# Rest blocks of the experts: 64 rows standing twice in the array instead of 128 rows once

## The chip, the cores and the metric

The kernel runs on one core of one Trainium2 chip. The metric is the device time of one execution in microseconds, lower is better; the median of several runs is compared. TensorE is called PE in the profile, its weight loads PEld, VectorE DVE, ScalarE ACT, GpSimd POOL and SyncE SP.

## The reference, cut to what matters

A decoder layer: causal self-attention, a mixing step over features, and a layer of 64 experts. Only the last part is touched. Each of the 4096 tokens goes to 8 experts; an expert computes a SiLU-gated product of two projections and projects it back, and the result is added to the token with its weight.

```python
logits = x @ gate_weight.T
top_val, top_idx = lax.top_k(softmax(logits), 8)        # 64 experts, 8 for each token
...
gu = lax.ragged_dot(xs, swapaxes(gate_up_proj, 1, 2), group_sizes)   # rows x 1024 by 1024 x 768
gate, up = jnp.split(gu, 2, axis=-1)
hact = jax.nn.silu(gate) * up
y = lax.ragged_dot(hact, swapaxes(down_proj, 1, 2), group_sizes)     # rows x 384 by 384 x 1024
out = zeros_like(x).at[tok].add(y * w[:, None])
```

4096 x 8 rows over 64 experts are 512 for each on average. Worked out from the reference and its inputs: 30 of the 64 experts get more than 512 rows. Their surplus over 512 is 145 rows for expert 0; 65, 95, 109 and 84 rows for experts 11, 29, 45 and 59; and 1 to 64 rows for the other 25. No expert is remapped.

## The kernel before, in words

All products are in fp32 made of two parts: a number is split into an upper part (`_hi`) and a remainder (`_lo`), and a product is three matmuls, upper by upper, upper by remainder, remainder by upper (`split_product`, L1931 to L1934).

The expert stage is `experts`. `for_experts` (L1802 to L1812) runs on each engine: for each expert one **super block** of 512 rows (`super_block`), then as many **rest blocks** (`tail_block`) as the expert has rows beyond 512, in pieces of 128 (`route` counts them into `blocks` and `starts`). Each engine's order is written out by hand, and engines meet only through semaphores.

A rest block on PE (L2024 to L2063): `first_layer(f)` for the three thirds f of the inner dimension, each 8 x 3 matmuls of 256 columns into `ps_gu` with the 128 rows as the stationary operand; `turn_h(f)` transposes the activation; `turn_tail` transposes the rows of the next gather (`xt_rows`); `second_layer(f)` makes 2 x 3 matmuls of 512 columns into `ps_y`. ACT makes the SiLU (L2163) and the upper parts of the transposed activation (L2168) and of the gathered rows (`split_tail`, L2085), DVE the product (L2355) and the remainders (L2359, L2259).

The result of a block leaves `ps_y` only when the next block runs: ACT scales it into `y_last` (`finish_last`, L2094), and POOL adds its 128 rows to `out` with one indirect DMA (`send_last`, L1897). The fourth piece of a super block goes the same way. POOL also gathers the rows of the next block (`gather_tail`, L1878). The row numbers of the send stand in `scatter_l`. DVE writes them for the next send as the last thing that it does in a rest block (L2375 to L2377), once `yl_sent` tells that the running send has landed.

After a rest block DVE goes on with the next expert, and the first thing there is the remainder `gu_lo` of its weights (`first_weights`, L2291), after ACT's upper part `gu_hi` (L2114). The first matmul of PE's next super block waits for the first piece of it.

The rows of each expert are listed on DVE in `table` (`finish_list`, L2218 to L2231), one column for each block of 128 rows.

## Time and profile before

| | us |
|---|---|
| median of 3 runs | 7708.75 (7703.13 to 7712.73) |
| profiled execution, its own time | 7711.42 |
| span of its instructions | 7709.8 |
| expert stage, from its first matmul | 3728.4 to the end |
| super blocks | 64 |
| rest blocks | 31 (93 transposes on L2044, three for each) |

The page gives each engine's busy time and the granted clock of PE in 40 slices of the span. The timeline gives single instructions with start and duration in us from the span's start, and in square brackets how long the engine was idle before and what released it. A duration of a matmul is longer than its distance to the next one, since matmuls are pipelined; what counts is the distance of the starts.

### The profile page before, as it was taken

Reading aid. Unit: us, or ns where it says so; the run is one execution under the profiler, and the core shown is the slowest. Engines: PE = TensorE matmul, PEld = TensorE weight load, DVE = VectorE, ACT = ScalarE, POOL = GpSimd, SP = SyncE. Lnnn points to the kernel's source line nnn. Section 1 sums busy time; section 2 is a strip of 40 time slices with the busy share of each in tenths; the row PEclk is TensorE's granted clock in tenths of the full one; section 3 lists DMA queues with packets and bytes.
Section 4 is the critical chain, followed back from the end, with each engine's and each line's share of the span. In section 5 each row is a group of like instructions: output and inputs, shape, how many; then the busy total and the mean of one; then the engine's idle time right before and its main releaser. Section 6 shows DMA issues by size and latency. Waiting matters only on the chain.

```text
span 7709.8 us, 118231 instructions
## 1 busy us (share of the span) xinstructions
PE 7148.1 (93%) x37743; PEld 5881.9 (76%) x37744; DVE 3972.6 (52%) x7056; ACT 3523.7 (46%) x6510; POOL 1815.6 (24%) x1602
## 2 busy tenths in 40 slices
PE   7998888898996899995799999999999999999999
PEld 5776776776775778784688888888888888888887
DVE  5666667666665443445444444444444444444444
ACT  4666676666665222120244444444444444444443
POOL 1122113113110000000233333333333333333333
PEclk9999999999998999996899999999999999999999
DMA  2111111112111222221465555556556565556555
GB/s 66 45 55 51 44 55 51 44 45 60 45 46 58 79 69 85 76 67 36 123 176 170 161 161 161 161 161 165 161 155 165 161 181 160 159 163 162 162 161 150
DMA packets 303596, 858.60 MB, mean 111 GB/s; under 512 B 42080, under 2 KB 83552, under 8 KB 303328
## 3 DMA queue, kind: packets, MB, share of 16 engines
q0 software_dynamic: 98928, 365.58, 20.3%
q1 hardware_dynamic: 204400, 489.67, 19.5%
q8 instruction: 142, 2.33, 0.1%
q14 instruction: 126, 1.03, 0.0%
HBM read 614.84 MB, written 206.70 MB: 107 GB/s over the span
## 4 chain that ended last, share of the span: by engine, by line
PE 52%; DVE 0%; POOL 0%; issue 0%; DMA 0%; ACT 0%; DVEq 0%; POOLq 0%
PE ps_gu L1932 10%; PE ps_gu L1934 10%; PE ps_gu L1933 10%; PE ps_y L1932 5%; PE ps_y L1934 5%; PE ps_y L1933 5%; PE ps_xe L1952 3%; PE ps_xe L1961 1%; PE ps_l L1941 1%; PE ps_h L2044 0%; DVE logits L2206 0%; DMA x_rows<-rows,gather_s 0%; DVE xs_lo L2252 0%; DVE at_hi L2199 0%; POOL x_rows L1869 0%
## 5 line engine op out<-in xcount | busy, mean ns | idle before, releaser
L1932 PE MATMUL ps_gu<-xs_hi,gu_hi 128*128 128x512 f32 x3072 | 1213.5, 395 | 7.3 <-DVE gu_lo L2291 7.3
L1934 PE MATMUL ps_gu<-xs_hi,gu_lo 128*128 128x512 f32 x3072 | 1207.0, 393 | 0.0
L1933 PE MATMUL ps_gu<-xs_lo,gu_hi 128*128 128x512 f32 x3072 | 1204.4, 392 | 0.0
L1911 POOL TENSOR_TENSOR dn_lo<-raw_w,dn_hi 128x512 fp32r<-128x512 f32 x384 | 485.0, 1298 | 947.0 <-ACT dn_hi L2114 947.0
L1932 PEld LDWEIGHTS ps_gu<-xs_hi,gu_hi 128*128 128x128 f32 x3072 | 577.8, 188 | 130.4 <-DVE gu_lo L2291 7.7
L461 PE MATMUL ps_qkv<-xt_hi,w_hi 128*128 128x512 f32 x1512 | 639.8, 423 | 37.7 <-ACT proj L614 30.0
L1933 PEld LDWEIGHTS ps_gu<-xs_lo,gu_hi 128*128 128x128 f32 x3072 | 578.1, 188 | 124.8
L1934 PEld LDWEIGHTS ps_gu<-xs_hi,gu_lo 128*128 128x128 f32 x3072 | 577.6, 188 | 125.3
L1932 PE MATMUL ps_y<-dn_hi,hs_hi 128*128 128x512 f32 x1536 | 628.6, 409 | 0.0
L893 DVE TENSOR_TENSOR pt_lo<-ps_t,pt_hi 128x512 fp32r<-128x512 f32 (+3 forms) x768 | 426.6, 555 | 391.9 <-ACT pt_hi L713 376.9
L644 ACT ACTIVATE probs<-ps_s,neg_max 128x128 f32<-128x128 f32 (+7 forms) x512 | 379.5, 741 | 506.6 <-DVE neg_max L824 505.7
L461 PE MATMUL ps_qkv<-xt_lo,w_hi 128*128 128x512 f32 x1512 | 610.6, 404 | 0.0
L2126 ACT ACTIVATE hs_hi<-act_s 128x512 fp32r<-128x512 f32 x192 | 121.3, 632 | 1067.8 <-DVE act_s L2301 1067.8
L461 PE MATMUL ps_qkv<-xt_hi,w_lo 128*128 128x512 f32 x1512 | 607.1, 402 | 0.0
L1934 PE MATMUL ps_y<-dn_hi,hs_lo 128*128 128x512 f32 x1536 | 606.6, 395 | 0.0
L1933 PE MATMUL ps_y<-dn_lo,hs_hi 128*128 128x512 f32 x1536 | 606.0, 395 | 0.0
L2301 DVE TENSOR_TENSOR act_s<-ps_gu,act_s 128x512 f32<-128x512 f32 x192 | 132.8, 691 | 894.2 <-PE ps_gu L1934 894.2
L2252 DVE TENSOR_TENSOR xs_lo<-ps_xe,xs_hi 128x512 fp32r<-128x512 f32 x520 | 334.3, 684 | 478.5 <-ACT xs_hi L2077 478.5
L1889 POOL DMA_INDIRECT out<-y_sup,scatter_s x192 | 303.1, 1579 | 1012.2 <-ACT y_sup L2136 983.1
L2291 DVE TENSOR_TENSOR gu_lo<-raw_w,gu_hi 128x512 fp32r<-128x512 f32 x768 | 485.1, 686 | 102.3 <-ACT gu_hi L2114 101.9
L2114 ACT ACTIVATE gu_hi<-raw_w 128x512 fp32r<-128x512 f32 x768 | 427.2, 620 | 218.7 <-DMA raw_w<-w_gu 159.8
L544 PE MATMUL ps_t<-ident,probs 128*128 128x128 f32 x2304 | 393.3, 281 | 78.5 <-ACT probs L652 54.9
(326 smaller groups left out, 15577.1 us busy)
## 6 DMA issues: line engine op xcount, KB each, us to landing
raw_w<-w_gu SPq DMA_DIRECT2D x384, 512.0 KB, 4.2
raw_w<-w_down SPq DMA_DIRECT2D x192, 512.0 KB, 6.3
w_raw<-wqkv SPq DMA_DIRECT2D x192, 256.0 KB, 2.7
turned<-proj SPq DMA_DIRECT2D x512, 64.0 KB, 2.0
out<-residual SPq DMA_DIRECT2D x36, 512.0 KB, 2.6
attn_out<-out_t POOLq DMA_DIRECT2D x128, 128.0 KB, 2.3
residual<-x SPq DMA_DIRECT2D x32, 512.0 KB, 5.3
stage<-attn_out SPq DMA_DIRECT2D x32, 512.0 KB, 5.8
```

The costliest lines, as they stand in the source:

```text
L461: mm = pe.matmul(out[:, :], ws[:, kind, k, :], xs[:, k, a], start=(n == 0), stop=(n == 3 * HB - 1))
L544: mm = pe.transpose(ps_t[:, (1 + at) % 2, i * P:(i + 1) * P], probs[g][:, i, kb * P:(kb + 1) * P], ident[:, :])
L644: act.activation(probs[g][:, i, 0:keys], ps_s[:, n % 2, 0:keys], ACT.Exp, bias=neg_max[:, n:n + 1], accum_out=row_sum[:, n:n + 1]).then_in ...
L893: dve.tensor_tensor(pt_lo[:, s % 2, off:], ps_t[:, (1 + at) % 2, off:], raw(pt_hi[:, s % 2, off:]), ALU.subtract).then_inc(tile_lo_ok, 1)
L1889: pool.indirect_dma_start(out, bass.IndirectOffsetOnAxis(ap=scatter_s[:, i:i + 1], axis=0), y_sup[:, i % 2, :], None, compute_op=ALU.add). ...
L1911: pool.tensor_tensor(dn_lo[:, f, a], raw_w[:, f, a], raw(dn_hi[:, f, a]), ALU.subtract).then_inc(dn_lo_ok, 1)
L1932: pe.matmul(out, a_hi, w_hi, start=first, stop=False)
L1933: pe.matmul(out, a_hi, w_lo, start=False, stop=False)
L1934: return pe.matmul(out, a_lo, w_hi, start=False, stop=last)
L2114: act.activation(dst[:, a], raw_w[:, c % RING, a], ACT.Copy).then_inc(hi_ok, 1)
L2252: dve.tensor_tensor(xs_lo[:, ks, a], ps_x1[:, c * BANK:(c + 1) * BANK].rearrange("p (k c) -> p k c", c=P), raw(xs_hi[:, ks, a]), ALU.subtr ...
L2291: dve.tensor_tensor(gu_lo[:, c // 2, b], raw_w[:, c % RING, a], raw(gu_hi[:, c // 2, b]), ALU.subtract).then_inc(lo_ok, 1)
```

## The change

The rows beyond 512 are now taken in rest blocks of 64. The 64 rows stand twice in the stationary operand of 128 columns, the upper part in columns 0 to 63 and the remainder in columns 64 to 127 (`xt`, `ht`). Two matmuls, one with the upper part of the weights and one with the remainder, replace three (`packed_product`). The two halves of the result lie on different partitions. After the first layer ACT copies the lower half out of PSUM (`lower_rows`) and DVE adds it to the upper half (`add_rows`) ahead of SiLU and product. After the second layer the halves are not added on chip: both stand in `y_last` and are added to the same rows of `out`. Therefore `send_last` sends partitions 0 to 63 only, and a new `send_second` waits until that has landed and then sends partitions 64 to 127. The fourth piece of a super block leaves by the same two sends. Each send counts 16 on `yl_sent`, so all waits for it now count 32 for a block. `table` has two columns for each former one with every entry on both halves of the partitions, and the gather fetches each of the 64 rows twice. On PE `turn_h(2)` now stands behind `second_layer(0)`. The reference's counts give 36 rest blocks in pieces of 64: 25 experts have one, four have two (before one), expert 0 has three (before two).

```diff
@@ route @@
-            after(dve.tensor_scalar(count[:, :], count[:, :], P - 1, None, ALU.add))
+            after(dve.tensor_scalar(count[:, :], count[:, :], P // 2 - 1, None, ALU.add))
...
-            after(dve.tensor_scalar(count[:, :], count[:, :], 7, None, ALU.arith_shift_right))
-            after(dve.tensor_scalar(blocks[:, :], count[:, :], float(SUP), 0.0, ALU.subtract, ALU.max))
+            after(dve.tensor_scalar(count[:, :], count[:, :], 6, None, ALU.arith_shift_right))
+            after(dve.tensor_scalar(blocks[:, :], count[:, :], float(2 * SUP), 0.0, ALU.subtract, ALU.max))
@@ experts, POOL @@
-                pool.indirect_dma_start(out, bass.IndirectOffsetOnAxis(ap=scatter_l[:, 0:1], axis=0), y_last[:, :], None,
+                pool.indirect_dma_start(out, bass.IndirectOffsetOnAxis(ap=scatter_l[0:T, 0:1], axis=0), y_last[0:T, :], None,
+                                        compute_op=ALU.add).then_inc(yl_sent, 16)
+
+            def send_second(n):
+
+                pool.wait_ge(yl_sent, LOADED + n * 32 + 16)
+                stand_alone(pool, passed)
+                pool.indirect_dma_start(out, bass.IndirectOffsetOnAxis(ap=scatter_m[:, 0:1], axis=0), y_last[T:P, :], None,
                                         compute_op=ALU.add).then_inc(yl_sent, 16)
...
                 for i in range(SUP):
                     gather_super(e + 1, i)
+                send_second(e + t0)
...
             def tail_block(e, t):
                 gather_tail(e + 1 + t)
                 send_last(e + 1 + t)
+                send_second(e + 1 + t)
@@ experts, PE @@
+            def packed_product(out, a, w_hi, w_lo, first, last):
+
+
+                both = a.rearrange("p a t -> p (a t)")
+                pe.matmul(out, both, w_hi, start=first, stop=False)
+                return pe.matmul(out, both, w_lo, start=False, stop=last)
...
-                        mm = split_product(ps_gu[:, f % 2, 0:W], xt_hi[:, a], xt_lo[:, a], gu_hi[:, f, c], gu_lo[:, f, c], k == 0, k == HB - 1)
+                        mm = packed_product(ps_gu[:, f % 2, 0:W], xt[:, k, :, :], gu_hi[:, f, c], gu_lo[:, f, c], k == 0, k == HB - 1)
...
+                second_layer(0)
                 turn_h(2)
-                second_layer(0)
                 second_layer(1)
@@ experts, ACT, tail_block @@
+                def lower_rows(f):
+
+
+                    act.wait_ge(tgu_ok, START + t * FB + f + 1)
+                    act.wait_ge(tsum_ok, START + t * FB + max(0, f - 1))
+                    act.activation(gu_low[:, f % 2, :], ps_gu[T:P, f % 2, 0:W], ACT.Copy).then_inc(tlow_ok, 1)
...
-                act.wait_ge(yl_sent, LOADED + n * 16)
+                act.wait_ge(yl_sent, LOADED + n * 32)
@@ experts, DVE, finish_list @@
-                dve.tensor_tensor(table[:, bass.ds(at + 1, N)], found[:, 0, :], found[:, 1, :], ALU.add).then_inc(list_ok, 1)
+                dve.tensor_tensor(table[:, bass.ds(at + 1, SUP)], found[:, 0, 0:SUP], found[:, 1, 0:SUP], ALU.add)
+                dve.tensor_tensor(found[:, 0, SUP:], found[:, 0, SUP:], found[:, 1, SUP:], ALU.add).then_inc(found_ok, 1)
...
+                    dve.tensor_copy(tails[0:T, :, half], rows_of)
+                    ins = dve.tensor_copy(tails[T:P, :, half], rows_of)
@@ experts, DVE, tail_block @@
+                def add_rows(f):
+
+                    dve.wait_ge(tlow_ok, START + t * FB + f + 1)
+                    dve.tensor_tensor(gu_sum[:, f % 2, :], ps_gu[0:T, f % 2, 0:W], gu_low[:, f % 2, :], ALU.add).then_inc(tsum_ok, 1)
...
-                dve.wait_ge(yl_sent, LOADED + (e + t + 2) * 16)
+                dve.wait_ge(yl_sent, LOADED + (e + t + 2) * 32)
                 stand_alone(dve, passed)
+                dve.tensor_copy(scatter_m[:, :], table[T:P, bass.ds((e + 1) * SUP + t + 1, 1)])
                 dve.tensor_copy(scatter_l[:, :], table[:, bass.ds((e + 1) * SUP + t + 1, 1)]).then_inc(sl_ok, 1)
```

On POOL a rest block has one gather and one send before. ISA rows are waits that take a register.

```order
L1875 REGISTER_ALU
L1878 DMA xt_rows<-rows,gather_t 128x1088
L1894 ISA
L1897 DMA out<-y_last,scatter_l 4608x1024
L1811 REGISTER_ALU
```

On POOL the same place after the change; L1906 is the wait for the landing of the first half.

```order
L1879 REGISTER_ALU
L1882 DMA xt_rows<-rows,gather_t 128x1088
L1898 ISA
L1901 DMA out<-y_last,scatter_l 4608x1024
L1906 ISA
L1908 DMA out<-y_last,scatter_m 4608x1024
L1814 REGISTER_ALU
```

A second send has come, and with it a wait between the two.

On DVE the end of a rest block before: remainder of the gathered rows, the wait for the send (L2375), the new row numbers.

```order
L2259 TENSOR_TENSOR xtail_lo<-ps_xe,xtail_hi 128x512 x2
L2375 ISA
L2377 ISA
L2377 COPY scatter_l<-table 128x1
L1811 REGISTER_ALU
```

On DVE the same place after; L2424 is the wait, which now asks for both sends of the block.

```order
L2298 TENSOR_TENSOR xtail<-ps_xe,xtail 128x4x64 x2
L2424 ISA
L2426 ISA
L2426 COPY scatter_m<-table 64x1
L2427 ISA
L2427 COPY scatter_l<-table 128x1
L1814 REGISTER_ALU
```

The order is the same but for one more copy; what the wait asks for has changed.

On PE the middle of a rest block after the change, behind the last matmul of `first_layer(2)`: `turn_h(1)` on L2064, `turn_tail` on L1982, then `second_layer(0)` ahead of `turn_h(2)`.

```order
L2064 MATMUL ps_h<-ident,act_t 128x128
L1978 ISA
L1979 ISA
L1982 MATMUL ps_xe<-ident,xt_rows 128x128 x8
L2070 REGISTER_ALU
L1954 MATMUL ps_y<-dn_hi,ht 128x512
L1955 MATMUL ps_y<-dn_lo,ht 128x512
L2070 REGISTER_ALU
L1954 MATMUL ps_y<-dn_hi,ht 128x512
L1955 MATMUL ps_y<-dn_lo,ht 128x512
L2062 REGISTER_ALU
L2064 MATMUL ps_h<-ident,act_t 128x128
```

Four matmuls of the second layer have moved ahead of the third transpose.

## Rows read from the trace of the kernel before

**Rows 1.** The page: PE's busy time, and its granted clock in 40 slices.

```profile
PE 7148.1 (93%) x37743; PEld 5881.9 (76%) x37744; DVE 3972.6 (52%) x7056; ACT 3523.7 (46%) x6510; POOL 1815.6 (24%) x1602
...
PEclk9999999999998999996899999999999999999999
```

**Rows 2.** Expert stage: stretch, length, busy PE, PEld, DVE, ACT, POOL; clock, DMA share, GB/s.

```profile
3735.00:7698.00 3963.00, 3962.68 (x21543) 3311.00 (x21541) 1838.05 (x3306) 1630.32 (x2990) 1291.98 (x1019) 1.00 0.59 163
```

**Rows 3.** Timeline of PE, a single rest block: start us, us, engine, line, instruction.

```profile
4462.66 0.28 PE L1932 MATMUL ps_gu<-gu_hi,xtail_hi 128*128 128x256 f32 x1
...
4468.12 0.27 PE L2044 MATMUL ps_h<-ident,act_t 128*128 128x128 f32 x1
...
4472.11 0.30 PE L2044 MATMUL ps_h<-ident,act_t 128*128 128x128 f32 x1
4472.22 0.49 PE L1932 MATMUL ps_y<-dn_hi,ht_hi 128*128 128x512 f32 x1
...
4476.51 0.40 PE L1932 MATMUL ps_gu<-xs_hi,gu_hi 128*128 128x512 f32 x1
```

**Rows 4.** Timelines of ACT, POOL and DVE in the same block.

```profile
4462.86 0.69 ACT L2094 ACTIVATE y_last<-ps_y,w_last 128x512 f32<-128x512 f32 x1 [1.41 <-PE ps_y L1934]
...
4464.38 1.56 POOL L1897 DMA_INDIRECT out<-y_last,scatter_l  x1 [1.78 <-ACT y_last L2094]
...
4474.80 0.14 DVE L2377 COPY scatter_l<-table 128x1 int32 x1
4475.19 1.29 DVE L2291 TENSOR_TENSOR gu_lo<-raw_w,gu_hi 128x512 fp32r<-128x512 f32 x2 [0.25 <-ACT gu_hi L2114]
```

**Rows 5.** Timelines of PE, DVE and POOL, around the second rest block of expert 0.

```profile
3797.61 0.14 DVE L2377 COPY scatter_l<-table 128x1 int32 x1
...
3798.76 0.99 POOL L1878 DMA_INDIRECT xt_rows<-rows,gather_t  x1 [10.19 <-DVE gather_t L2245]
...
3799.33 0.28 PE L1932 MATMUL ps_gu<-gu_hi,xtail_hi 128*128 128x256 f32 x1
...
3813.27 0.40 PE L1932 MATMUL ps_gu<-xs_hi,gu_hi 128*128 128x512 f32 x1
```

**Rows 6.** Groups by form, attention: the same sizes from PSUM; last numbers busy us, mean ns.

```profile
L893 DVE TENSOR_TENSOR pt_lo<-ps_t,pt_hi 128x256 fp32r<-128x256 f32 x128 | 54.1, 422 | 15.3 <-ACT pt_hi L713 14.4
L713 ACT ACTIVATE pt_hi<-ps_t 128x256 fp32r<-128x256 f32 x128 | 48.5, 379 | 16.0 <-PE ps_t L544 14.3
```

**Rows 7.** Tile `y_last`, landing of the sends issued at 4464.4 and at 4588.6 us.

```profile
DMA to landing us min/median/max: 6.5/6.5/6.5
...
DMA to landing us min/median/max: 8.1/8.1/8.1
```

**Rows 8.** Tile `y_sup`, landing of a send of 128 rows issued at 5831.9 us.

```profile
DMA to landing us min/median/max: 6.4/6.4/6.4
```

**Rows 9.** Two stretches of that send; the last two numbers are DMA share and GB/s.

```profile
5831.90:5833.90 2.00, 2.00 (x10) 1.62 (x9) 2.00 (x3) 0.99 (x2) 1.61 (x1) 1.00 0.00 0
5833.90:5835.90 2.00, 2.00 (x14) 1.67 (x13) 0.32 (x1) 0.58 (x2) 0.00 (x0) 1.00 0.96 106
```

**Rows 10.** The page, DMA issues: name, count, KB each, us to landing.

```profile
attn_out<-out_t POOLq DMA_DIRECT2D x128, 128.0 KB, 2.3
```

**Rows 11.** Timeline of PE, the first matmul behind an idle stretch in the mixing step.

```profile
3274.38 0.80 PE L1110 MATMUL ps_b<-at_hi,split 128*128 128x512 f32 x1 [4.90 <-DVE split L1433]
```

**Rows 12.** Windows behind two idle stretches of 4.90 us; third from the right is the clock.

```profile
2764.48:2769.20 4.72, 4.72 (x11) 3.76 (x12) 2.20 (x2) 0.00 (x0) 0.00 (x0) 0.50 0.91 268
3274.40:3277.80 3.40, 3.40 (x8) 2.73 (x9) 2.18 (x2) 0.00 (x0) 0.00 (x0) 0.50 0.97 312
```

**Rows 13.** Timeline of DVE in the super block behind.

```profile
4506.12 0.14 DVE L2340 COPY scatter_l<-scatter_s 128x1 int32<-128x1 int32 x1
4511.69 0.69 DVE L2301 TENSOR_TENSOR act_s<-ps_gu,act_s 128x512 f32<-128x512 f32 x1 [5.42 <-PE ps_gu L1934]
```

**Rows 14.** Timeline of POOL, the last send of the program.

```profile
7699.30 1.55 POOL L1897 DMA_INDIRECT out<-y_last,scatter_l  x1 [3.61 <-ACT y_last L2094]
```

More of the change, by code:

```diff
@@ L1730, in experts @@
     TOKENS = SUP * P
-    TAILS = N * TOPK
+    T = P // 2
+    TAILS = 2 * N * TOPK
+    LISTED = SUP + 2 * (N - SUP)
     with ExitStack() as scope:
@@ L1742, in experts @@
         xs_lo = m.sb("xs_lo", [P, HB, TOKENS], F32R)
-        xt_hi = m.sb("xtail_hi", [P, H], F32R)
-        xt_lo = m.sb("xtail_lo", [P, H], F32R)
+        xt = m.sb("xtail", [P, HB, 2, T], F32R)
+        gu_low = m.sb("gu_low", [T, 2, W])
+        gu_sum = m.sb("gu_sum", [T, 2, W])
         act_s = m.sb("act_s", [P, TOKENS])
@@ L1762, in experts @@
         scatter_l = m.sb("scatter_l", [P, 1], I32)
-        table = m.sb("table", [P, 1 + TAILS + SUP * (E + AHEAD) + N], I32)
+        scatter_m = m.sb("scatter_m", [T, 1], I32)
+        table = m.sb("table", [P, 1 + TAILS + SUP * (E + AHEAD) + LISTED], I32)
         own = m.sb("own", [P, 1])
@@ L1790, in experts @@
         gt_ok, xt_ps, xt_hi_ok, xt_lo_ok, wtn_ok = (m.sem(n) for n in ("gt_ok", "xt_ps", "xtail_hi_ok", "xtail_lo_ok", "wtn_ok"))
-        tgu_ok, tsilu_ok, tprod_ok, th_ps, th_hi_ok, th_lo_ok = (
-            m.sem(n) for n in ("tgu_ok", "tsilu_ok", "tprod_ok", "th_ps", "th_hi_ok", "th_lo_ok"))
+        tgu_ok, tlow_ok, tsum_ok, tsilu_ok, tprod_ok, th_ps, th_hi_ok, th_lo_ok = (
+            m.sem(n) for n in ("tgu_ok", "tlow_ok", "tsum_ok", "tsilu_ok", "tprod_ok", "th_ps", "th_hi_ok", "th_lo_ok"))
         yl_ps, yl_ok, wl_ok, sl_ok = (m.sem(n) for n in ("yl_ps", "yl_ok", "wl_ok", "sl_ok"))
@@ L1860, in _ @@
             pool.iota(scatter_l[:, :], [[0, 1]], base=0, channel_multiplier=1).then_inc(set_up, 1)
+            pool.iota(scatter_m[:, :], [[0, 1]], base=T, channel_multiplier=1).then_inc(set_up, 1)
             def gather_super(n, i):
@@ L2167, in split_h @@
                     act.wait_ge(yl_ps, START + (e + 1 + t) * 2 + 2)
-                    act.activation(ht_hi[:, f, :], ps_h[:, f * P:(f + 1) * P], ACT.Copy).then_inc(th_hi_ok, 1)
+                    act.activation(ht[:, f, 0, :], ps_h[:, f * P:f * P + T], ACT.Copy).then_inc(th_hi_ok, 1)
                 finish_last(e + 1 + t)
+                lower_rows(0)
                 silu_of(0)
+                lower_rows(1)
                 silu_of(1)
                 split_h(0)
+                lower_rows(2)
                 silu_of(2)
@@ L2187, in _ @@
             dve.memset(warm[:, :], 0.0).then_inc(set_up, 1)
+            dve.memset(act_t[:, :, :], 0.0).then_inc(set_up, 1)
             dve.memset(w_now[:, :], 0.0).then_inc(set_up, 1)
             dve.memset(w_last[:, :], 0.0).then_inc(wl_ok, 1)
-            dve.wait_ge(set_up, START + 13)
+            dve.wait_ge(set_up, START + 15)
             stand_alone(dve, sl_ok)
@@ L2227, in finish_list @@
                                          op0=ALU.is_equal, op1=ALU.mult).then_inc(found_ok, 1)
-                dve.wait_ge(found_ok, START + n + 1)
+                dve.wait_ge(found_ok, START + n * 2 + 1)
                 at = tails_before(dve, n) + n * SUP
-                dve.tensor_tensor(table[:, bass.ds(at + 1, N)], found[:, 0, :], found[:, 1, :], ALU.add).then_inc(list_ok, 1)
+                dve.tensor_tensor(table[:, bass.ds(at + 1, SUP)], found[:, 0, 0:SUP], found[:, 1, 0:SUP], ALU.add)
+                dve.tensor_tensor(found[:, 0, SUP:], found[:, 0, SUP:], found[:, 1, SUP:], ALU.add).then_inc(found_ok, 1)
+                dve.wait_ge(found_ok, START + n * 2 + 2)
+                tails = table[:, bass.ds(at + 1 + SUP, 2 * (N - SUP))].rearrange("p (n a) -> p n a", a=2)
+                for half in range(2):
+                    rows_of = found[half * T:(half + 1) * T, 0, SUP:]
+                    dve.tensor_copy(tails[0:T, :, half], rows_of)
+                    ins = dve.tensor_copy(tails[T:P, :, half], rows_of)
+                ins.then_inc(list_ok, 1)
                 dve.wait_ge(list_ok, START + n + 1)
@@ L2337, in super_block @@
                 dve.tensor_copy(w_last[:, :], w_now[:, SUP - 1:SUP]).then_inc(wl_ok, 1)
-                dve.wait_ge(yl_sent, LOADED + (e + t0 + 1) * 16)
+                dve.wait_ge(yl_sent, LOADED + (e + t0 + 1) * 32)
                 dve.wait_ge(ss_ok, START + e + 1)
+                dve.tensor_copy(scatter_m[:, :], scatter_s[T:P, SUP - 1:SUP])
                 dve.tensor_copy(scatter_l[:, :], scatter_s[:, SUP - 1:SUP]).then_inc(sl_ok, 1)
```

39 lines of the change are left out of this document (21 added, 18 removed).

## The prediction

> **What bounds the kernel now.** Read the page first: PE is busy for 7148 of 7710 us, and its clock is at the upper level nearly throughout [rows 1]. Then the stage that is touched, by a window: from 3735 to 7698 us PE is busy for 3962.7 of 3963.0 us [rows 2]. No other engine is over half. So in this stage PE's work is the time, and whatever makes PE wait is added at full price. Third, one rest block in the timelines. Its first matmul starts at 4462.66 and the next super block's at 4476.51, so it takes 13.85 us [rows 3]. The second block of expert 0 takes 13.94 us [rows 5]. I take 13.9 for each of the 31. Below, all times of a block count from its first matmul.
>
> **What the change takes from PE.** The 48 matmuls of `first_layer(0)` and `(1)` take 5.46 us, from 4462.66 to the transpose at 4468.12. The 24 of `first_layer(2)` take 2.73 at the same pitch. The 18 of the second layer take 4.29, from 4472.22 to 4476.51 [rows 3]. Of these 12.5 us two thirds stay, 8.3. With the transposes, which stay (some 1.4 us), a block of 64 rows is 9.7 us of work. The blocks become 36. If nothing waited, the rest would cost 36 x 9.7 = 349 instead of 31 x 13.9 = 431 us: 82 us less. That is the gain on paper.
>
> **What it adds inside the block.** `turn_h(0)` now waits for ACT's copy, the addition, SiLU and the product: a copy and an addition of 256 columns, 0.38 and 0.42 us by their like [rows 6], then two steps half as wide, 1.6 us with the hops between them, under `first_layer(1)`, which lasts 1.85 us. For `turn_h(2)`, `turn_h(1)`, `turn_tail` and `second_layer(0)` lie over the same chain, 2 us. Both just fit; I put 0 on them, at most 0.3 us each.
>
> **What it adds behind the block, and this decides.** DVE's last work in a block is `scatter_l`, for which it waits until the running send has landed. What is queued behind that wait on DVE is `gu_lo` of the next expert, and PE's next super block waits for its first piece. Before, the send starts at 1.72 us, 0.83 us after ACT has finished `y_last` (4463.55 to 4464.38) [rows 4]. It lands 6.5 to 8.1 us later [rows 7], so at 8.2 to 9.8, and DVE comes to its wait only at 12.1 [rows 4]: it costs nothing. The cover is 2.3 us or more, and two edits remove it. The block shrinks by 4.2 us, and the send becomes two, one behind the other.
>
> How long do 64 rows take to land? No row shows it. A send of 128 rows alone lands after 6.4 us [rows 8]. In its first 2.0 us nothing moves; in the next 2.0 us 106 GB/s do, which is 212 KB of its 512 [rows 9]. So half of the bytes have moved at about 4.3 us, and what follows takes some 0.5 us: about 4.8 us for a half, 1.6 less than for the whole. The first half shares the queue with the gather ahead of it, as the whole did: 7.2 (midway in rows 7, and a little less) minus 1.6 is 5.6. The bounds are far apart. Below, a plain POOL transfer of 128 KB lands in 2.3 us [rows 10]; above, a half may cost as much as a whole, 7.2 and 6.4. I take 5.6 and 4.8, since rows 8 and 9 are the same operation with the same kind of rows.
>
> The chain is then: 1.72 + 5.6 + 0.83 (POOL from a release to its next send) + 4.8 = 13.0 us. From `scatter_l` to the end of the first piece of `gu_lo` it was 1.1 us (4474.80 to 4475.19 plus half of 1.29) [rows 4]. With the second copy, the wake-up and PE's start that is 1.4, so PE begins the super block at **14.4 us** instead of 13.9. PE's own work was over at 9.7. The whole gain of a block is gone, and 4.7 us of idle PE stand in its place.
>
> There is a floor below that, even with instant sends. `turn_h(2)` at 4472.11 is followed by ACT's `split_h`, `split_tail`, its loop end and `gu_hi`, then `gu_lo`, whose first piece ends at 4475.8: 3.7 us [rows 3, 4]. With half-sized `split_tail` it is 3.4. `turn_h(2)` now starts at about 7.7, so PE can't begin before 11.1.
>
> **Two rest blocks in a row.** The second one starts on PE at 9.7, but DVE is released only at 13.0, and gather and send come behind it. From `scatter_l` to POOL's gather it was 1.15 us [rows 5]: gather at 14.4, 1.0 long, next send at 15.7. Behind the gather its first half needs 5.2, then 0.83 and 4.8: 26.5, and PE's super block starts at 27.9. PE's work, with its waits for SiLU and gather, ends at about 23.5 and is hidden under that. So an extra block costs 27.9 - 14.4 = 13.5 us.
>
> **The clock.** PE now idles for 4.7 us once per expert with a rest. Elsewhere in this trace PE idles for 4.90 us and then works at the lower of its two levels, 1.2 instead of 2.4 GHz: 0.50 is granted over 4.7 us in one place and over 3.4 us in the other, where the first matmul takes 0.80 us [rows 11, 12]. Half of such a stretch is lost: 2.4 and 1.7, I take 1.9 us, 30 times. Between 0 and 2.4 is possible.
>
> **Where there is cover.** In the super block the fourth piece also leaves in two sends. The second is issued behind the gathers, some 11 us into the block, and DVE needs it at 4506.1, 29.6 us into the block. The five small instructions more in `finish_list` come out of the 5.42 us that DVE idles before its next product [rows 13]. 0 for both. At the end of the program nothing covers: the last send at 7699.3 [rows 14] lands after 6.4 before, after 4.8 + 0.83 + 4.8 = 10.4 now, 4.0 more. A longer `iota` and a memset ahead of the stage: 1, by their size, and 0 to 2.
>
> **The sum.** 25 experts with one block: 25 x (14.4 - 13.9) = 12. Four with two instead of one: 4 x (27.9 - 13.9) = 56. Expert 0, three instead of two: 14.4 + 2 x 13.5 - 2 x 13.9 = 14. Clock: 30 x 1.9 = 57. End and start: 5. Together 144 us on 7711.4, the profiled execution, which is 2.7 above the median: **7853 us**.
>
> **The rivals.** (1) The same without the clock: PE is fed soon enough or the gap is judged otherwise. 7709 + 87 = 7796. For it speaks that in the expert stage no drop is seen; there is no gap there either. 12%. (2) *Faster*: the halves land quickly, as rows 10 would have it. If the two landings together are under some 6.5 us, only the floor of 11.1 is left: 25 x (11.1 - 13.9) = -70, four pairs 4 x (9.7 + 11.1 - 13.9) = +28, expert 0 19.4 + 11.1 - 27.8 = +3, end 1: 7670. Without clock losses the sum changes its sign where the two landings sum up to 8.2 us instead of 10.4. Against it stand rows 7 to 9. 7%. (3) *Much slower*: a half costs as much as a whole, 1.72 + 7.2 + 0.83 + 6.4 = 16.2 and 17.6 for a block. Each of the 36 then costs 3.2 more than in my sum, 115; with 2.4 for the clock and 7 at the end 7985. 7%. (4) The number of blocks stays 31 (the counts don't come out as the reference says, or most surplus fits one block anyway): 31 x 0.5 + 57 + 5, so 7786. 3%. My forecast: 71%.
>
> The Trainium skill, page "DMA: Bandwidth & Descriptors", section "Anatomy of one DMA — SWDGE (gpsimd) path", fits a POOL-issued DMA as a fixed 2.0 us plus its bytes over 436 GB/s. By it a half of 256 KB would be an estimated 2.6 us, the chain would end at 7.8 us, under PE's work, and rival 2 would hold. The trace disagrees for the same DMA in whole: 3.2 us by that rule, 6.4 to 8.1 measured [rows 7, 8].
>
> **How the numbers follow.** The likeliest case is 7853. The range has to take in the landing times (each us more or less in the chain is 36 us) and the clock (0 to 72 us), and leaves out rivals 2 and 3: **7785 to 7925**. About 0.2%, 15 us, is what a measurement of this kernel can tell from no change. Faster 0.07 (rival 2), same 0.03 (between rivals 1 and 2), slower 0.90.
>
> **What would show it.** Right: in the timeline after a rest block PE idles for about 4 us until `gu_lo`, 30 times, some 130 us in the waits; DVE's copy `scatter_m` starts at 13 us, at the landing of the second send; the page has 202 sends of `y_last` with landings near 5 us, 36 x 3 transposes on `ps_h`; the first matmuls of those super blocks are longer, and the granted clock of the window in rows 2 falls from 1.00 to about 0.98. Wrong: if DVE's copies follow `xtail` at once, the sends are not the bound; if PE waits inside the block (before `ps_h`), the new chain through ACT and DVE is longer than its cover; if PE idles as told and the clock stays up, rival 1.

## The result and the profile after

The changed kernel takes **7835.9 us** in the median of 4 runs (7824.7 to 7837.7), the kernel before 7706.1 in the same comparison: a ratio of **1.0164**, 95% interval 1.0147 to 1.0182. It is slower by 1.6%, inside the predicted range and 17 us under the predicted time.

The page of the kernel after, PE's busy time and its granted clock in 40 slices, against [rows 1]:

```profile
PE 7127.5 (91%) x37096; PEld 5837.9 (75%) x37098; DVE 4307.2 (55%) x7644; ACT 3545.1 (45%) x6655; POOL 1971.3 (25%) x1711
...
PEclk9999999999997999995999999999999999999999
```

PE has 647 instructions less to do, and the span is 7835.7 instead of 7709.8 us. The window over the expert stage, where [rows 2] had 3962.68 us of work in 3963.00 us, and a second one behind one rest block (stretch, length, busy PE, PEld, DVE, ACT, POOL; clock, DMA share, GB/s):

```profile
3735.00:7824.00 4089.00, 3938.66 (x20873) 3262.90 (x20871) 2168.26 (x3876) 1650.72 (x3134) 1444.47 (x1123) 0.98 0.58 158
4494.46:4501.29 6.83, 4.79 (x11) 3.79 (x12) 4.41 (x11) 2.67 (x5) 3.03 (x3) 0.50 0.47 89
```

PE is now idle for 150 us of the stage, and the clock of the stage is 0.98 instead of 1.00. Which wait is it? The waits of the stage (who waited for whom: us in total, times, longest):

```profile
POOL out L1908 <- DMA out<-y_last,scatter_l: 163.5, 36, 6.2
...
PE ps_gu L1946 <- DVE gu_lo L2331: 125.3, 30, 5.4
DVE scatter_m L2426 <- DMA out<-y_last,scatter_m: 91.9, 35, 3.9
```

30 times PE waits for `gu_lo`, once per expert with a rest block; DVE waits for the second half of a send, 35 times; POOL waits for the first half ahead of the second, 36 times. The other 25 us of PE's idle time are smaller things: waits inside the blocks, which the part on the sizes comes back to, and gaps too short for this view. One block shows the chain. Timeline of PE, where L1955 is the last matmul of the rest block and L1946 begins the super block:

```profile
4492.00 0.40 PE L1955 MATMUL ps_y<-dn_lo,ht 128*128 128x512 f32 x1
4496.50 0.79 PE L1946 MATMUL ps_gu<-xs_hi,gu_hi 128*128 128x512 f32 x1 [4.10 <-DVE gu_lo L2331]
4497.09 0.63 PE L1947 MATMUL ps_gu<-xs_lo,gu_hi 128*128 128x512 f32 x1
```

Timelines of ACT, POOL and DVE in the same block, against [rows 4]:

```profile
4482.61 0.69 ACT L2114 ACTIVATE y_last<-ps_y,w_last 128x512 f32<-128x512 f32 x1 [1.41 <-PE ps_y L1948]
...
4492.73 2.19 ACT L2134 ACTIVATE gu_hi<-raw_w 128x512 fp32r<-128x512 f32 x4 [1.39 <-issue]
```

```profile
4484.12 1.45 POOL L1901 DMA_INDIRECT out<-y_last,scatter_l  x1 [1.78 <-ACT y_last L2114]
4489.97 1.42 POOL L1908 DMA_INDIRECT out<-y_last,scatter_m  x1 [4.40 <-DMA out<-y_last,scatter_l]
```

```profile
4494.96 0.15 DVE L2426 COPY scatter_m<-table 64x1 int32 x1 [2.53 <-DMA out<-y_last,scatter_m]
4495.12 0.15 DVE L2427 COPY scatter_l<-table 128x1 int32 x1
4495.75 2.55 DVE L2331 TENSOR_TENSOR gu_lo<-raw_w,gu_hi 128x512 fp32r<-128x512 f32 x4 [0.48 <-issue]
```

The tile `y_last`, landing of the two sends of this block:

```profile
DMA to landing us min/median/max: 5.1/5.1/5.1
...
DMA to landing us min/median/max: 4.8/4.8/4.8
```

The block's first matmul is at 4482.41, and all that follows counts from there, in us: first send 1.71, landed 6.8, second send 7.56, landed 12.3, DVE free 12.55, `gu_lo` 13.34, super block 14.09. ACT has the first `gu_hi` ready at 10.9 (4492.73 plus a quarter of 2.19) and PE has ended at 10.0; both wait for DVE. Then the first matmuls take 0.79 and 0.63 us instead of 0.40, with 0.50 granted in the second window above.

### The profile page after: what moved, and what is told of

It reads as the page before. It is cut to its first block, busy times and chain, and to the rows that moved or that the text cites. A ratio compares the mean times of both kernels' runs of the same rounds, so it can differ in the third digit from the quotient of the medians.

```text
span 7835.7 us, 118818 instructions
## 1 busy us (share of the span) xinstructions
PE 7127.5 (91%) x37096; PEld 5837.9 (75%) x37098; DVE 4307.2 (55%) x7644; ACT 3545.1 (45%) x6655; POOL 1971.3 (25%) x1711
## 4 chain that ended last, share of the span: by engine, by line
PE 46%; DMA 4%; issue 1%; DVE 1%; ACT 0%; DVEq 0%; POOL 0%; POOLq 0%; ACTq 0%
PE ps_gu L1946 9%; PE ps_gu L1948 9%; PE ps_gu L1947 9%; PE ps_y L1946 5%; PE ps_y L1948 5%; PE ps_y L1947 5%; PE ps_xe L1973 3%; DMA out<-y_last,scatter_l 2%; DMA out<-y_last,scatter_m 2%; PE ps_l L1962 1%; PE ps_xe L1982 1%; DVE gu_lo L2331 0%; ACT y_last L2114 0%; DVE logits L2237 0%; DMA x_rows<-rows,gather_s 0%
## 5 line engine op out<-in xcount | busy, mean ns | idle before, releaser
L1946 PE MATMUL ps_gu<-xs_hi,gu_hi 128*128 128x512 f32 x3072 | 1242.6, 405 | 133.5 <-DVE gu_lo L2331 133.5
L1948 PE MATMUL ps_gu<-xs_hi,gu_lo 128*128 128x512 f32 x3072 | 1229.1, 400 | 0.0
L1947 PE MATMUL ps_gu<-xs_lo,gu_hi 128*128 128x512 f32 x3072 | 1225.9, 399 | 0.0
L1946 PEld LDWEIGHTS ps_gu<-xs_hi,gu_hi 128*128 128x128 f32 x3072 | 592.9, 193 | 271.8 <-DVE gu_lo L2331 147.0
L1946 PE MATMUL ps_y<-dn_hi,hs_hi 128*128 128x512 f32 x1536 | 628.5, 409 | 0.0
L369 POOL TENSOR_TENSOR w_lo<-w_raw,w_hi 128x512 fp32r<-128x512 f32 x192 | 261.7, 1363 | 852.6 <-ACT w_hi L598 852.5
```

What stands on the lines that cost most here:

```text
L369: pool.tensor_tensor(w_lo[:, i // 2, a, :], w_raw[:, i % RAWS, :, :], raw(w_hi[:, i // 2, a, :]), ALU.subtract).then_inc(w_lo_ok, 1)
L1946: pe.matmul(out, a_hi, w_hi, start=first, stop=False)
L1947: pe.matmul(out, a_hi, w_lo, start=False, stop=False)
L1948: return pe.matmul(out, a_lo, w_hi, start=False, stop=last)
```

## Experiments

Four kernels first: take the suspected wait off its place, keep PE's clock up and leave the wait, make the two sends without the rest of the change, and a first try at a better kernel.

**1. The row numbers of a send are written in the block that sends.** This moves the wait from ahead of `gu_lo` to a place where the send has long landed, except between two rest blocks; the same is done in the super block.

```
             def tail_block(e, t):
+                rows_of_send(...)   # wait for the send before; scatter_m; scatter_l
                 add_rows(0)
...
-                dve.wait_ge(yl_sent, LOADED + (e + t + 2) * 32)
-                stand_alone(dve, passed)
-                dve.tensor_copy(scatter_m[:, :], table[T:P, ...])
-                dve.tensor_copy(scatter_l[:, :], table[:, ...]).then_inc(sl_ok, 1)
```

> The row numbers of a send are written by DVE at the start of the block whose products are sent, no longer at the end of the block before, where DVE waits for both halves of the send to have landed ahead of the gate's remainder gu_lo. Nothing of the computation is changed. My theory (the super block behind a rest block begins when the second half of the send has landed and DVE has then written gu_lo; in the changed kernel 14.1 us after the rest block's start in the median): DVE is free of the send, gu_lo follows the gate's values, and the super block begins some 11.2 us after the rest block's start; 30 times 2.9 us are 87 us, and TensorE's idle time ahead of it falls from 4.1 to some 1.2 us, with which most of the 62 us that the low clock costs go too: 7690 to 7750 us, likeliest 7700. Rival (the chain within the rest block, or the weights' conversion, sets the super block's begin, and the wait for the send only lies beside it): within 15 us of 7836.

Measured: 7717.8 us, against 7709.4 of the kernel before in the same comparison, ratio 1.0015 (1.0005 to 1.0025). One edit that removes no work brings back 118 of 130 us. The waits of its expert stage, and a single block on DVE and PE; this block begins at 4467.89:

```profile
PE ps_gu L1946 <- DVE gu_lo L2330: 54.7, 30, 2.2
```

```profile
4478.79 2.50 DVE L2330 TENSOR_TENSOR gu_lo<-raw_w,gu_hi 128x512 fp32r<-128x512 f32 x4 [0.90 <-ACT gu_hi L2134]
4482.15 0.15 DVE L2340 COPY scatter_m<-table 64x1 int32 x1 [0.86 <-issue]
```

```profile
4479.53 0.51 PE L1946 MATMUL ps_gu<-xs_hi,gu_hi 128*128 128x512 f32 x1 [1.66 <-DVE gu_lo L2330]
```

`gu_lo` comes first now and the copies behind it, and it waits for ACT, not for a landing. Of DVE's wait for the second landing 13.1 us are left, 5 times, at the start of an expert's second and third blocks. The super block begins at 11.6 in this block and at 12.0 in the median of 30, not at 11.2 as expected: the floor was set too low, the cause was right. Only 3 stretches with a lower clock are left in the expert stage, where the changed kernel has 30.

**2. The same wait, but PE kept at work through it.**

```
+            def keep_busy(e):
+                pe.wait_ge(list_id, START + e + AHEAD + 1)
+                for i in range(18):
+                    pe.matmul(ps_l[:, :], iota_lo[:, :], row_base..., start=True, stop=True)
```

> The changed kernel with 18 matmuls of 128x512 bf16 more on TensorE behind each expert's last rest block, whose result nothing reads: they fill the idle time ahead of the super block and change nothing else. My theory (the idle time of some 4.1 us ahead of the super block lets the clock fall, and the super blocks behind it take 2.07 us longer each, 62 us in all): all super blocks take 55.2 us again, the granted clock of the expert stage is 1.00, and the time is 7836 less 62, 7774 us, or up to 15 us more where the matmuls run past the begin of the super block. Rival (the super blocks are longer because something they wait for is late, and the clock has no part in it): 7830 to 7850.

Measured: 7778.9 us, ratio 1.0096 (1.0079 to 1.0112). Timeline of PE behind one rest block, and the window of the expert stage:

```profile
4483.79 3.83 PE L2092 MATMUL ps_l<-row_base,iota_lo 128*128 128x512 bf16 x17
4487.81 0.50 PE L1948 MATMUL ps_gu<-xs_hi,gu_hi 128*128 128x512 f32 x1 [0.18 <-DVE gu_lo L2338]
```

```profile
3735.00:7640.00 3905.00, 3875.31 (x20789) 3176.09 (x20817) 2103.59 (x3765) 1600.00 (x3046) 1401.88 (x1090) 1.00 0.59 161
```

The blocks are as long as in the changed kernel (14.0 in the median), DVE's wait for the second landing is the same (87.7 us in all over this window, 89.3 in the changed kernel), and yet 57 us are gone (7835.9 to 7778.9) with more work on PE. So the clock alone is worth 57 of the 130 us, and the idle time that PE has in the changed kernel is what lowers it. A super block behind a rest block takes 55.3 us in the mean here, as in the kernel before (55.3), where the changed kernel has 57.3.

**3. The kernel before, with its send in two.**

```
-  pool.indirect_dma_start(out, ... scatter_l[:, 0:1] ..., y_last[:, :], ...)
+  pool.indirect_dma_start(out, ... scatter_l[0:64, 0:1] ..., y_last[0:64, :], ...)
+  # send_second: wait until it has landed, then
+  pool.indirect_dma_start(out, ... scatter_m[:, 0:1] ..., y_last[64:128, :], ...)
```

> The kernel before with its send of 128 rows given as two sends of 64 rows, one after the other has landed, and nothing else of the change: rest blocks still hold 128 rows, three weight passes. My theory (two sends cost only where the super block waits for them: here the first half's landing of 5.1 us, POOL's 0.8 and the second's 4.7 end about where the sequence of TensorE's 13.9 us does, since the send starts at 1.7): the super block begins at most 0.5 us later, no low clock in the expert stage, 7710 to 7725. Rival (two sends cost by themselves, through POOL, the DMA queues or the weights' loads, wherever they lie): 7770 or more.

Measured: 7720.0 us, ratio 1.0014 (1.0005 to 1.0024), 11 us over the kernel before, of which 5 come at the end of the program, where the two sends lie bare. The waits of its expert stage:

```profile
DVE scatter_m L2390 <- DMA out<-y_last,scatter_m: 8.3, 15, 1.9
PE ps_gu L1944 <- DVE gu_lo L2303: 4.3, 8, 1.7
```

The second send lies under 13.85 us of matmuls. DVE waits 8.3 us in all instead of 91.9, PE 4.3 instead of 125.3. From a rest block to the super block it is 0.26 us longer in the mean than in the kernel before. The same two sends cost next to nothing under a long block and hold up what follows a short one: what counts is how long they are against the block, not the second send by itself.

**4. A try at more: shorter way to the last conversion.** On top of experiment 1, ACT and DVE split the gathered rows of the next block (`split_tail`, `rest_of_tail`) before they split the last third of `h`, and the list's numbers are made int32 ahead of the four copies.

```
                 split_h(1)
+                split_tail(e + 1 + t, t + 1)
                 split_h(2)
-                split_tail(e + 1 + t, t + 1)
...
-  dve.tensor_tensor(found[:, 0, SUP:], ...)
+  dve.tensor_tensor(found_i[:, :], ...)
```

> As the first run, and two changes more: the remainder pass of the rest block's activations is made ahead of the last conversion of the next block's halves on ACT and DVE, and the list's row numbers are added straight into an int32 tile, so that the four casts behind it read whole numbers instead of a float tile (1.1 us each now). My theory (with the wait for the send gone, the chain within the rest block bounds it): some 20 us less than the first run by the order, and 3 us less by the casts ahead of the first expert, about 7680. Rival (the first run is bound by the weights' conversion for the super block): no difference to the first run but the 3 us.

Measured: 7709.3 us, ratio 1.0003 (0.9993 to 1.0013), equal to the kernel before. It gave 9 us against experiment 1 instead of 23, and the intervals of the two ratios overlap, so even the 9 are known to a few us only. Both halves of my expectation missed. The groups of DVE for the four copies, first the changed kernel (source f32), then this one (source int32); busy us, mean ns:

```profile
L2268 DVE CAST table<-found 64x28 f32 x128 | 158.7, 1240 | 1.7
L2267 DVE CAST table<-found 64x28 f32 x128 | 146.4, 1144 | 10.3
```

```profile
L2268 DVE COPY table<-found_i 64x28 int32 x128 | 159.0, 1242 | 1.7
L2267 DVE COPY table<-found_i 64x28 int32 x128 | 147.1, 1149 | 9.9
```

The type of the source is not what makes them long. And the block: ACT, from its last `ht` to the first weights, in a block that begins at 4461.64, and the chain of work that ended last, in the same stretch (`ACTq` is ACT's sequencer, L1804 reads an expert's count of rest blocks, and there are two of them):

```profile
4469.92 0.22 ACT L2196 ACTIVATE ht<-ps_h 128x64 fp32r<-128x64 f32 x1 [0.28 <-PE ps_h L2065]
4471.86 2.19 ACT L2135 ACTIVATE gu_hi<-raw_w 128x512 fp32r<-128x512 f32 x4 [1.72 <-issue]
```

```profile
4470.44 0.29 ACTq L1804
...
4470.76 0.15 ACTq L1804
...
4471.07 0.28 ACTq L1804
...
4471.38 0.16 ACTq L1804
```

`gu_hi` begins 10.2 us into the block, as it did in experiment 1, although the arithmetic ahead of it ends 0.4 us earlier. What the profile calls "issue" on ACT is its sequencer, which reads the two counts after it has issued the last instruction of the block, 1.15 us for both (4470.44 to 4471.59). That was new to me, and the next kernels test it.

**5. ACT reads its second count behind the super block.** Experiment 4 with that edit.

```
                 t0 = tails_before(eng, e)
-                t1 = tails_before(eng, e + 1)
                 super_block(e, t0, ...)
+                t1 = tails_before(eng, e + 1)
```

> The fourth run with change (2) alone: ACT reads its second count behind the super block. My theory (the counts' loads are on the chain): ACT begins gu_hi 0.6 us earlier and the super block too, 30 times 0.6 us are 18 us, 7691 us. Rival (the loads only fill a wait for something else): the begin of gu_hi stays 10.2 us behind the block's, 7709 us.

Measured: 7694.2 us, ratio 0.9982 (0.9973 to 0.9992). ACT and PE in a block that begins at 4466.10:

```profile
4474.25 0.23 ACT L2199 ACTIVATE ht<-ps_h 128x64 fp32r<-128x64 f32 x1 [0.27 <-PE ps_h L2068]
4475.57 2.19 ACT L2138 ACTIVATE gu_hi<-raw_w 128x512 fp32r<-128x512 f32 x4 [1.09 <-issue]
```

```profile
4477.41 0.50 PE L1950 MATMUL ps_gu<-xs_hi,gu_hi 128*128 128x512 f32 x1 [1.33 <-DVE gu_lo L2334]
```

ACT's gap went from 1.72 to 1.09 us, and `gu_hi` from 10.2 to 9.5 into the block. The total fell by 15 us (18 expected). It comes apart differently than I had said, though. In the profiled executions the ways from a rest block to the super block are 7 us shorter together, and 12 us come from super blocks, of which only one stretch has the lower clock now.

**6. PE begins with the products that need no remainder.** Experiment 5, and PE multiplies `gu_hi` with both parts of the rows before it needs `gu_lo`; the list's numbers go through a tile of fixed place.

```
+  for k in range(0, HB, 2):
+      pe.wait_ge(hi_ok, ...)
+      for q in (k, k + 1):   # gu_hi * xs_hi, gu_hi * xs_lo
+      pe.wait_ge(lo_ok, ...)
+      for q in (k, k + 1):   # gu_lo * xs_hi
```

> As the fourth run, and three changes more. (1) TensorE multiplies the first weights' upper parts with both parts of the super block's rows as soon as ACT has rounded them, and adds the products with the remainder gu_lo for two k at a time behind that, so that it begins one DVE pass (0.69 us) earlier. (2) ACT reads the second of its two counts (L1804) behind the super block and not ahead of it, where the two loads stand between its last rounding of the rest block and its first of the weights (1.1 of 1.7 us idle). (3) The four copies that write the list's rows go into a tile of fixed place, which one copy brings into the table. My theory (in the fourth run the super block waits for ACT's counts, gu_hi and gu_lo in a row, which end 1.5 us behind TensorE): the wait falls to 0.4 us, 30 times 1.1 us are 33 us, and the last low clock goes, 4 us: some 7672 us; the copies of (3) take 1.1 us each as before if the stride of their target is what costs, 0.2 us if it is the address from a register. Rival (something else than this chain sets the begin, at 10.2 us into the block in all of the runs so far): within 5 us of 7709.

Measured: 7692.5 us, ratio 0.9980 (0.9971 to 0.9989): against experiment 5 nothing, where 20 us were expected. Timeline of PE, and of the line that reads the counts, in a block that begins at 4465.97 and whose last matmul of 0.40 us starts at 4475.55 (`PEldq` is PE's sequencer):

```profile
4477.31 0.49 PE L2016 MATMUL ps_gu<-xs_hi,gu_hi 128*128 128x512 f32 x1 [1.36 <-ACT gu_hi L2150]
```

```profile
L1805 PEldq TENSOR_LOAD <-starts x2: 306/350/393, 4475.4 to 4476.2; - x2
```

The profile names `gu_hi`, but its first piece, which is all that this matmul needs, had long been there: ACT began the four pieces at 4475.43 and the first of them takes some 0.55 us. PE's own sequencer was late: it reads its two counts between 4475.4 and 4476.8 and comes to the super block's instructions behind that. Each engine reads the counts for itself, and PE's reading had been hidden as long as something else was later. The copies, by group:

```profile
L2282 DVE COPY turned_rows<-found_i 64x28 int32<-64x28 int32 x128 | 159.0, 1243 | 1.7
...
L2285 DVE COPY table<-turned_rows 128x56 int32 x64 | 12.3, 192 | 9.4
```

With a target of fixed place they take 1.24 us as before, while one copy of 56 numbers in a row takes 0.19 with its place from a register. So it is not the register. What is left of what I tried is the target's stride of two numbers; a target without a stride but else the same wasn't tried.

**7. The second send left out.** The changed kernel, where the lower half of each rest block's rows isn't added to the result.

```
             def send_second(n):
-                pool.wait_ge(yl_sent, LOADED + n * 32 + 16)
-                stand_alone(pool, passed)
-                pool.indirect_dma_start(out, ... scatter_m ..., y_last[T:P, :], ...)
+                pass
```

All waits for a landing now ask for 16 a block instead of 32; nothing else differs.

> The changed kernel without the second send: the lower half of each rest block's rows isn't added to the result, all else is as it was, the order of DVE's steps too. My theory (it is the second half's landing that DVE waits for ahead of gu_lo): DVE is free when the first has landed, 6.5 to 7.5 us into the block; the super block begins at some 11.8 us as in the run with the row numbers written late, and the end is one send shorter: about 7715 us. Rival (the wait is only where it is since DVE or ACT are late otherwise): within 20 us of 7836.

Measured: 7683.8 us, ratio 0.9972 (0.9961 to 0.9983). DVE and PE in a block that begins at 4451.10:

```profile
4461.13 0.15 DVE L2423 COPY scatter_m<-table 64x1 int32 x1
...
4461.99 2.50 DVE L2328 TENSOR_TENSOR gu_lo<-raw_w,gu_hi 128x512 fp32r<-128x512 f32 x4 [0.55 <-ACT gu_hi L2131]
```

```profile
4462.74 0.51 PE L1943 MATMUL ps_gu<-xs_hi,gu_hi 128*128 128x512 f32 x1 [1.67 <-DVE gu_lo L2328]
```

DVE's steps stand in the changed kernel's order, and yet it does not wait; the super block begins at 11.65 (11.8 expected). So the second landing is the wait. The total is 31 us lower than I said, since I had taken it from experiment 1. The two profiled spans differ by 38.6 us: 9.6 ahead of the expert stage, where the code is the same (its first product comes at 3718.4 instead of 3728.0), 13.9 in rest blocks (the ways to the super block take 11.69 us in the mean instead of 12.08, extra blocks 10.35 instead of 10.79), 11.7 in super blocks, which have no low clock here, and 3.4 at the end, one send shorter.

**8 and 9. Counts read inside the super block, with and without the early products.** Both stand on experiment 4. PE and ACT read both counts behind their first products and first conversions. For that, two waits go that were covered already: PE's for `tprod_ok` (its last `turn_h` waited for the same) and ACT's for `tgu_ok`.

```
             with eng.Fori(0, E) as e:
...
-                t0 = tails_before(eng, e)
-                t1 = tails_before(eng, e + 1)
-                super_block(e, t0, t1)
+                t0, t1 = super_block(e)     # PE: behind first_layer(0, 1); ACT: behind split(1)
```

> The run of the fourth kernel, with three changes: the early products of (1); TensorE and ACT read both of their counts (L1804, loads of 0.31 to 0.36 us and the steps behind them, 1.5 us of TensorE's own sequencer ahead of the first matmul) inside the super block, behind its first products and first conversions; and two waits go that an earlier wait of the same engine already covers. The copies of (3) are as in the fourth run. My theory (the last 1.5 us ahead of the super block are TensorE's sequencer, which reads both counts there, whatever ACT and DVE do; that is why the early products gained nothing): the idle time ahead of the super block falls below 0.3 us, a rest block and its way to the super block take 9.9 to 10.2 us, 30 times 1.4 us are 42 us: some 7650 us. Rival (the weights' conversion sets it): no idle time below 0.9 us, 7680 or more.

> As the run beside it without the early products. My theory: TensorE's sequencer is early, but gu_hi and then gu_lo have to be there; ACT begins gu_hi some 0.8 us behind its last ht (4474.4 in a block that ends at 4475.95), gu_lo ends 1.3 us later: idle time of about 0.7 us and 7665 us, between the runs on either side. Rival (the products' order counts for nothing, sequencer alone): the same time as the run beside it, within 3 us.

Measured with both: **7639.6 us, ratio 0.9915 (0.9901 to 0.9928)**. Without the early products: 7658.3 us, ratio 0.9940 (0.9924 to 0.9955). Both are a little faster than expected, by 10 and 7 us. Timelines of PE, first with both, in a block that begins at 4453.01, then without the early products:

```profile
4462.74 0.40 PE L1959 MATMUL ps_y<-dn_lo,ht 128*128 128x512 f32 x1
4462.98 0.39 PE L2014 MATMUL ps_gu<-xs_hi,gu_hi 128*128 128x512 f32 x1
```

```profile
4459.95 0.51 PE L1950 MATMUL ps_gu<-xs_hi,gu_hi 128*128 128x512 f32 x1 [0.48 <-DVE gu_lo L2338]
```

With both edits the super block follows without a gap, 10.0 us into this block and 9.8 in the median, and that is what the prediction put down as PE's bare work (9.7). Without the products a block takes 10.5 in the median, 0.65 us more, and PE is idle for 0.48 us ahead of the super block, where about 0.7 had been expected. The edit that gave nothing in experiment 6 gives 19 us here: it was right and stood behind another wait.

**10. Are these edits good for either form?** The kernel before with both of them.

> The kernel before, with the early products and with TensorE's and ACT's counts read inside the super block, as in the run of 7640 us, and nothing of the change. My theory (a rest block of 128 rows takes TensorE 13.85 us of matmuls, and the super block follows on its last one without a gap, so these edits have nothing to give there; what they give, they give only to blocks of 64 rows): 7700 to 7706 us. Rival (the edits help either form, and the change of the rest blocks has no part in the 67 us): 7690 or less.

Measured: 7702.1 us, ratio 0.9998 (0.9988 to 1.0007). The window of its expert stage:

```profile
3735.00:7640.00 3905.00, 3904.98 (x21243) 3263.03 (x21242) 1808.04 (x3261) 1611.11 (x2950) 1274.04 (x1003) 1.00 0.59 163
```

PE is without a gap, as before. The 67 us of experiment 8 come from the change of the rest blocks, once nothing stands between a block's end and the super block. The edits of experiments 1 and 4 were not tried on the kernel before; they only move waits, and PE has none there to lose (3962.68 us of work in 3963.00 us, [rows 2]).

## Why the prediction was right, and where its sizes were off

**The cause** stood as predicted, at each of its steps: POOL's second send waits for the first landing, DVE's copies for the second, `gu_lo` is queued behind them, PE waits 30 times. Experiments 1 and 7 take the wait away in two ways and give the same block (12.0 and 11.65); experiment 3 shows that the sends cost nothing while the block is long, experiment 2 what part the clock has.

**The chain of one block.** Predicted 1.72 + 5.6 + 0.83 + 4.8 = 13.0 and the super block at 14.4; measured (the block of 4482.41, to two places from the same trace) 1.71 + 5.06 + 0.79 + 4.75 = 12.3, DVE free at 12.55, super block at 14.1. The first half's landing was the term that was too large, by 0.5: it had been worked out as a whole send's 7.2 less 1.6. The way that a whole send divides its time into a stretch without bytes and one with them [rows 9] gave the second half's 4.8 to the tenth. The 1.4 behind it were too small: from the landing to the super block it is 1.8. The two errors partly cancel, which is luck: 0.7 too late at the landing, 0.3 too late at the super block. By the Trainium skill, page "DMA: Bandwidth & Descriptors", section "Anatomy of one DMA — SWDGE (gpsimd) path", a half would have landed after an estimated 2.6 us, which is the prediction's rival 2; this case's trace disagrees, with 4.8 and 5.1.

**The sum**, in us, of the profiled executions (7709.8 and 7835.7 us of span):

| term | predicted | measured |
| --- | --- | --- |
| experts with one block | 25: +12 | 26: +5 |
| experts with two | 4: +56 | 3: +44 |
| expert 0, three | +14 | +15 |
| the clock | 30 x 1.9 = +57 | 30 x 2.07 = +62 |
| end, start | +4, +1 | +5.9, +3.1 |
| ahead of the stage, same code | 0 | -8.8 |
| together | +144 | +126 |

That the sum came out 18 us too high, and not further off, is in part luck. The experts with one and two blocks cost 19 us less than predicted, 14 of them because one expert has one block instead of two, and 8.8 us come from code that the change doesn't touch. Against these, expert 0, the clock, the end and the start together cost 10 us more than predicted.

- *Number of blocks.* I took 36 from the reference; the chip has 35. L2064 runs three times a block:

```profile
L2064 PE MATMUL ps_h<-ident,act_t 128*128 128x128 f32 x105 | 30.3, 288 | 5.7 <-DVE act_t L2401 5.7
```

One expert, number 11, which has 577 rows by the reference, stays within 576 here: in the trace only expert 0 (three blocks) and experts 29, 45 and 60 (two each) have more than one. (The expert with a surplus of 84 is 60; the list ahead calls it 59.) That is rival 4 for one expert of five, and it is worth 14 us. That its count lay one row above the border was there to be seen.

- *Two blocks in a row.* Predicted 27.9 us until the super block, measured 28.2 from 5619.51, where the first of this pair begins, and 27.8 and 30.0 in the other two; the timeline of PE in the second block:

```profile
5638.77 1.06 PE L1982 MATMUL ps_xe<-ident,xt_rows 128*128 128x128 f32 x8 [1.50 <-DMA xt_rows<-rows,gather_t]
...
5647.67 0.79 PE L1946 MATMUL ps_gu<-xs_hi,gu_hi 128*128 128x512 f32 x1 [4.92 <-DVE gu_lo L2331]
```

- *Inside the block*: I put 0 on the new steps. The second of two blocks begins on PE at 10.4 in three experts of four (11.8 in the last), not at 9.7. The longer chain to `act_t` does outlast its cover in second and third blocks; the waits of the stage have

```profile
PE ps_xe L1982 <- DMA xt_rows<-rows,gather_t: 10.7, 9, 1.8
PE ps_h L2064 <- DVE act_t L2401: 5.7, 5, 2.3
```

All five of the second line, and 9 us of the first, fall to experts with more than one block, where they lie under the sends. In the 26 single blocks only three such waits are longer than 0.1 us (0.3 to 0.6 us each, for the gathered rows); experiment 8 shows 9.8 for such a block where nothing is behind.

- *`finish_list`.* "Five small instructions" was wrong in size: four of them take 1.04 to 1.24 us each. They did come out of DVE's idle time, as said, so the price was 0 in the super blocks; ahead of the first expert, where nothing covers them, they are in the 3.1 us of the start. I had priced them by their number of elements and not looked for a row with such a target.

- *The clock.* 1.9 lay between two stretches elsewhere (1.7 and 2.4); 2.07 was measured in the mean of 30 and 57 us in all by experiment 2. Rival 1 (no clock, 7796) is thereby out for the changed kernel, and nearly what experiment 2 built.

- *The end*: the last two sends, timeline of POOL, take 4.7 us to land each. From the first issue to the last landing it is 10.2 us, where the single send of [rows 14] took 6.4. From the last landing to the end of the span it is 6.3 us instead of 4.2, which the prediction had not counted: the trace shows a DRAIN on POOL's sequencer there that lasts 5.5 us instead of 3.4. In experiment 7, without a second send, it lasts 7.3 us, so the second send isn't needed to make it longer; the cause stays open.

```profile
7819.29 1.42 POOL L1901 DMA_INDIRECT out<-y_last,scatter_l  x1 [3.60 <-ACT y_last L2114]
7824.79 1.42 POOL L1908 DMA_INDIRECT out<-y_last,scatter_m  x1 [4.07 <-DMA out<-y_last,scatter_l]
```

- *The landings.* The page has 200 sends of `y_last`, two for each of 100, and they are near 5 us only in the rest blocks: 4.7 to 6.8 us for the first half (5.2 in the median), 4.5 to 4.9 for the second. In the super blocks the second half takes up to 11.3 us (9.6 in the median). Nothing waits for it there: the waits for a second half, 35 of DVE and 13 of ACT, all stand behind the sends of rest blocks. So the 0 for that place held, although the landing is twice as long as I had taken a half to be.

- *Ahead of the stage.* 8.8 us less in code that is the same in both, between two executions. No run shows why. The beginning of the stage lies between 3718 and 3730 us in the twelve profiles of this case, so a comparison of single spans is no better than that.

**The floor** of 11.1 us, on which rival 2 rested, was too low by some 0.5 to 0.9: experiments 1 and 7 have 12.0 and 11.65. I had counted ACT's "loop end" by one row of before and not seen what it consists of. Had the two landings been short, the time would have been near 7718, as in experiment 1, and not 7670: rival 2 was not only unlikely, its price was wrong too. So was its border: a floor of 11.1 is reached where the two landings sum to 11.1 - 1.72 - 0.83 - 1.4 = 7.15 us, not 6.5. They sum to 9.8. The paper gain of 82 us was real: experiment 8 gets 67 of it.

## What to carry to other kernels

When a stage on a full engine gets shorter, list everything that ran in its shadow, with its end counted from the stage's start (here a send of two landings, 12.3 us, and each engine's loads of loop counts, 1.2 to 1.5 us): the gain stops at the longest of them. Put a wait for a transfer where its result is needed and not where the last step happens to stand, since all that the engine has queued behind it waits too. If an edit gives nothing, keep it and look again once the wait in front of it is gone: the early products were worth 0 and later 19 us.

## What the runs showed of the hardware that I had not expected

- In the rest blocks sends that add 64 rows of 4 KB land after 4.5 to 4.9 us (the second half) or 4.7 to 6.8 (the first, behind a gather), where 128 rows took 6.1 to 8.3 before: in halves the same data takes 9.9 us and a further 0.8 of POOL between them (medians 5.2 and 4.7 against 7.5). In the super blocks a half takes up to 11.3 us.
- A sequencer that reads a count from memory takes 0.28 to 0.39 us for the load in the blocks looked at here (0.30 in the median of all loads of the changed kernel, single ones up to 0.81) and nearly as much again for the steps behind it; PE, ACT, POOL and DVE each do it for themselves. It shows as "issue" on ACT, and on PE as a wait for whatever came last.
- DVE's copy of 64x28 numbers to every second place of an int32 tile takes 1.04 to 1.24 us, from float or from int32, to a fixed place or to one from a register; 128x56 numbers in a row take 0.19.
- The 30 idle stretches of PE ahead of a super block in the changed kernel (3.6 to 5.4 us, 4.1 in the median) were all followed by the lower clock; of those in experiment 1 (1.65 to 2.2 us) 3 of 30 were.
